# Gated linear attention on TensorE: state products with 64 rows per head in two banks instead of block-diagonal states

## The reference, cut to what matters

```
z = cumlogsumexp(s, axis=time);  g = exp(z_prev - z);  p = exp(s - z)
hk = hk * g + k (x) p            # state of 64 x 64 a head
ok = q . hk;  pv = softmax(ok)
hv = hv * g + p (x) v            # state of 64 x 128 a head
o = pv . hv
```

## Time and profile before

| | us |
|---|---|
| median of 3 runs (lowest, highest) | 891.55 (891.05, 891.7) |
| profiled execution, its own time | 890.84 |
| its span, slowest core (core 4) | 889.3 |
| even cores | 887.1 to 889.3 |
| odd cores | 856.3 to 859.7 |
| TensorE busy, core 4 | 845.4 |
| VectorE, ScalarE, GpSimd busy, core 4 | 364.0, 343.2, 150.8 |

### The profile page before, as it was taken

One profiled execution on the slowest core, in us unless ns is written; L12 is line 12 of the kernel. 1 busy time (PEld: TensorE's weight loads), 2 busy tenths in 40 slices (PEclk: granted clock), 3 DMA queues, 4 the chain that ended last, 5 costly groups with the idle time before them and its releaser, 6 DMA issues.

```text
span 889.3 us, 15119 instructions; the slowest of 8 cores (856.3 to 889.3 us)
## 1 busy us (share of the span) xinstructions
PE 845.4 (95%) x5521; PEld 455.7 (51%) x5585; DVE 364.0 (41%) x862; ACT 343.2 (39%) x746; POOL 150.8 (17%) x196
## 2 busy tenths in 40 slices
PE   3899999999999999999999999999999999999992
PEld 1344555555555555555555554444445666655540
DVE  1121244554555545454555554455553000023344
ACT  0111246555656456555655555101122222223333
POOL 6000012211222112112121222002112000001113
PEclk9899999999999999999999999999999999999997
DMA  8999902240422314221540226937703910005224
GB/s 136 161 171 169 162 1 48 49 83 14 96 48 48 65 32 95 49 48 28 116 95 1 84 56 172 268 87 136 149 1 77 181 29 1 1 14 129 95 95 193
DMA packets 13617, 77.46 MB, mean 87 GB/s; under 512 B 1632, under 2 KB 1632, under 8 KB 6624
## 3 DMA queue, kind: packets, MB, share of 16 engines
q0 software_dynamic: 9504, 57.51, 36.3%
q1 hardware_dynamic: 4032, 18.90, 5.5%
HBM read 124.47 MB, written 9.44 MB: 151 GB/s over the span
## 4 chain that ended last, share of the span: by engine, by line
PE 93%; DMA 2%; issue 2%; DVE 1%; ACT 1%; POOL 1%; POOLq 0%; DVEq 0%; ACTq 0%
PE p L246 64%; PE no L246 19%; PE tb L246 4%; PE aw L246 4%; DMA ws_a<-wsp 2%; PE st L246 1%; ACT sqd_a L293 0%; POOL xfm_a L300 0%; DVE x_a L266 0%; ACT mv_a L290 0%; POOL x_a L1208 0%; POOL ws_a L300 0%; POOLq L1348 0%; DVE x_a L1160 0%; DVE vx_a L266 0%
## 5 line engine op out<-in xcount | busy, mean ns | idle before, releaser
L246 PE MATMUL p<-s_a,xfm_a 128*128 128x512 bf16 x1117 | 253.0, 379 | 1.8
L246 PEld LDWEIGHTS p<-s_a,xfm_a 128*128 128x128 bf16 x1152 | 111.2, 98 | 123.9
L550 POOL TENSOR_TENSOR ng_a<-ng_a,gt_a 128x512 f32<-128x512 f32 x36 | 45.8, 1271 | 300.4 <-ACT gt_a L290 241.2
L246 PE MATMUL p<-x2fm_a,s_a 128*128 128x384 bf16 x512 | 87.5, 326 | 0.0
L266 DVE TENSOR_TENSOR awm_a<-aw,cbs 128x1024 bf16<-128x1024 f32 (+1 forms) x38 | 44.4, 1168 | 99.7 <-PE aw L246 99.7
L246 PE MATMUL p<-s_a,ofm_a 128*128 128x512 bf16 x341 | 78.2, 379 | 3.3 <-DVE x_a L266 2.8
L246 PE MATMUL p<-xfm_a,wq_a 128*128 128x384 bf16 x384 | 66.2, 326 | 0.0
L246 PEld LDWEIGHTS p<-x2fm_a,s_a 128*128 128x128 bf16 x512 | 48.4, 97 | 32.1 <-issue 0.6
L246 PE MATMUL p<-xfm_a,wk_a 128*128 128x384 bf16 x384 | 64.4, 326 | 0.0
L246 PEld LDWEIGHTS p<-s_a,ofm_a 128*128 128x128 bf16 x352 | 33.7, 98 | 40.7 <-issue 2.9
L246 PE MATMUL no<-s_a,ofm_a 128*128 128x512 bf16 x219 | 50.7, 379 | 0.3
(11 more groups left out here) (150 smaller groups left out, 1094.4 us busy)
## 6 DMA issues: line engine op xcount, KB each, us to landing
s_a<-w1p POOLq DMA_DIRECT2D x10, 1024.0 KB, 14.2
x_a<-x_main SPq DMA_DIRECT2D x9, 1024.0 KB, 12.2
s_a<-wvp POOLq DMA_DIRECT2D x8, 1024.0 KB, 17.1
s_a<-wgp POOLq DMA_DIRECT2D x8, 1024.0 KB, 11.9
s_a<-wop POOLq DMA_DIRECT2D x8, 1024.0 KB, 13.1
y<-x_a SPq DMA_DIRECT2D x16, 512.0 KB, 2.7
xfm_a<-xt_main POOLq DMA_DIRECT2D x12, 384.0 KB, 25.7
ws_a<-wsp POOLq DMA_DIRECT2D x8, 512.0 KB, 30.1
```

Source lines behind the costliest of these rows:

```text
L246: return t.matmul(out, lhsT, rhs, start=start, stop=stop, is_transpose=tp, skip_group_check=skip)
L550: g_tok[it] = gop(lambda e: e.tensor_tensor(b, b, gt.ap(0, 512), ALU.mult), [sg, n])
```

## The change

`s1bd` and `s2bd` become `s1` (128 columns) and `s2` (256 columns), in which the two heads of a pair lie below each other in the partitions and nothing is zero. The copies out of `st` become one instruction each. Each state product becomes two, of 64 rows of contraction, for the heads `e` = 0 and 1; these write to two banks. Numerators and denominators move from NP to `aw` (bank `e`, columns 0 to 127 and 128 to 255); the denominators become products of 128 columns, two for each before. The outputs use both banks of `no`. The instructions that read them take both banks with one access pattern, and the order of heads in `rr`, `okb`, `sm4` and `rs4` becomes that of the banks; the transposed order is undone in writing `cbf` and `ot`. `aw` is now freed by `sm_max` also, and both banks of `no` by `dve_ot`. The two `wo_unit` behind the loop use the two banks of `aw`.

```diff
-    s1bd = [small(f"s1bd{i}", 256, BF16) for i in range(2)]
-    s2bd = [small(f"s2bd{i}", 512, BF16) for i in range(3)]
+    s1 = [small(f"s1{i}", 128, BF16) for i in range(2)]
+    s2 = [small(f"s2{i}", 256, BF16) for i in range(3)]
...
-    for i in range(2):
-        z = v_set(s1bd[i].ap(0, 256), 0.0)
-    for i in range(3):
-        z = v_set(s2bd[i].ap(0, 512), 0.0)
...
-        a = v_copy(s1bd[b].ap3(0, [[128, 2], [1, 64]], 0, 64),
-                   bass.AP(ST, S1O, [[512, 64], [64, 2], [1, 64]]), w + [z])
-        a = v_copy(s1bd[b].ap3(64, [[128, 2], [1, 64]], 64, 64),
-                   bass.AP(ST, 64 * 512 + S1O, [[512, 64], [64, 2], [1, 64]]), w)
+        a = v_copy(s1[b].ap(0, 128), ST[:, S1O:S1O + 128], w)
...
+        q = s_copy(s2[it % 3].ap3(0, [[128, 2], [1, 128]]),
+                   bass.AP(ST, 0, [[512, 128], [S2O, 2], [1, 128]]), [m, a, o_mm.get(it - 3)])
...
     def pe_num_den(it):
         g, c = divmod(it, NM)
         b = it % 2
         eg = c * 1024 + g * GW
-        mm(NP[:, 256:512], lmask, em.ap(eg, 256), True, False, [t_e, t_cb] + fr(NP))
         before = c > 0 or NPF
-        if before:
-            mm(NP[:, 256:512], ones_bf, dg[b].ap(0, 256), False, False, [st_dg[it]])
+        for e in range(2):
+            mm(AW2[:, e * 512 + DEN:e * 512 + DEN + 128], lmask, em.ap3(eg + 64 * e, [[128, 2], [1, 64]]),
+               True, False, [t_e, t_cb] + fr(AW2) if e == 0 else [], skip=True)
+        for e in range(2 if before else 0):
+            mm(AW2[:, e * 512 + DEN:e * 512 + DEN + 128], ones_bf, dg[b].ap3(64 * e, [[128, 2], [1, 64]]),
+               False, False, [st_dg[it]] if e == 0 else [], skip=True)
         for p in range(2 if before else 0):
-            mm(NP[:, p * 128:(p + 1) * 128], kq[g % 2].ap((2 + p) * TM + c * 128, 128),
-               s1bd[b].ap(p * 128, 128), False, False, [st_s1[it]] if p == 0 else [])
-        for h in range(4):
-            p, e = divmod(h, 2)
-            tok = mm(NP[:, h * 64:h * 64 + 64], awm.ap(e * 512 + AOFF + p * 128, 128),
-                     em.ap(eg + h * 64, 64), False, h == 3, [a_tok[it]] if h == 0 else [], inc=(h == 3))
+            for e in range(2):
+                o = e * 512 + p * 64
+                mm(AW2[:, o:o + 64], kq[g % 2].ap((2 + p) * TM + c * 128, 128, 64 * e, 64),
+                   s1[b].ap(p * 64, 64, 64 * e, 64), False, False, [st_s1[it]] if p + e == 0 else [], skip=True)
+        for p in range(2):
+            for e in range(2):
+                o = e * 512 + p * 64
+                tok = mm(AW2[:, o:o + 64], awm.ap(e * 512 + AOFF + p * 128, 128),
+                         em.ap(eg + (2 * p + e) * 64, 64), False, True, [a_tok[it]] if p + e == 0 else [],
+                         inc=(p + e == 2), skip=True)
...
-        o1 = v_tt(okb.ap(0, 256), NP[:, 0:256], rr.ap(0, 256), ALU.mult, [r2, tok])
-        set_free(NP, o1, r2)
+        o1 = v_tt(okb.ap3(0, [[128, 2], [1, 128]]), pair(AW2, 0, 128), rr2, ALU.mult, [r2, tok])
+        set_free(AW2, o1, r2)
...
     def pe_outputs(it):
         before = it % NM > 0 or NPF
         for p in range(2 if before else 0):
-            mm(OB[:, p * 256:(p + 1) * 256], cT[it % 2].ap(p * 128, 128), s2bd[it % 3].ap(p * 256, 256),
-               p == 0, False, [st_s2[it], ct_tok[it]] + fr(OB) if p == 0 else [])
...
+            for e in range(2):
+                o = e * 512 + p * 128
+                mm(NO2[:, o:o + 128], cT[it % 2].ap(p * 128, 128, 64 * e, 64), s2[it % 3].ap(p * 128, 128, 64 * e, 64),
+                   p == 0, False, [st_s2[it], ct_tok[it]] + out_free["o"] if p + e == 0 else [], skip=True)
...
     dve_ot(last)
+    for half in AW:
+        set_free(half, *fr(AW2))
+    rot[0] = 1
     for _ in range(2):
         cc, n = wo_list.pop(0)
-        wo_unit(cc, n, gen[:3])[1]()
+        wo_unit(cc, n, AW)[1]()
+    for half in (NP, OB):
+        set_free(half, *out_free["o"])
     b_ot = pe_ot(last)
     act_of(last, b_ot)
```

More of the change, by code:

```diff
@@ L712, in dve_masks, with pair @@
             a_tok[ai] = t
+    DEN = 128
+    out_free = {"o": []}
+    def pair(h, lo, n):
+        return bass.AP(h, lo, [[1024, 128], [512, 2], [1, n]])
     def pe_num_den(it):
@@ L732, in emit @@
     ok3 = okb.ap3(0, [[64, 4], [1, 64]])
+    rr2 = rr.ap3(0, [[128, 2], [1, 128]])
     def sm_den(it, tok):
-        r1 = s_act(rr.ap(0, 256), NP[:, 256:512], AF.Ln, waits=[tok, c_tok.get(it - 1)])
+        r1 = s_act(rr2, pair(AW2, DEN, 128), AF.Ln, waits=[tok, c_tok.get(it - 1)])
         return s_act(rr.ap(0, 256), rr.ap(0, 256), AF.Exp, scale=-1.0, waits=[r1])
     def sm_max(it, tok, r2):
-        o1 = v_tt(okb.ap(0, 256), NP[:, 0:256], rr.ap(0, 256), ALU.mult, [r2, tok])
-        set_free(NP, o1, r2)
+        o1 = v_tt(okb.ap3(0, [[128, 2], [1, 128]]), pair(AW2, 0, 128), rr2, ALU.mult, [r2, tok])
+        set_free(AW2, o1, r2)
         o2 = v_red(mx4.ap(0, 4), ok3, ALU.max, [o1], negate=True)
@@ L747, in sm_end @@
     def sm_end(it, ex):
-        s1 = v_red(sm4.ap(0, 4), ok3, ALU.add, [ex])
-        s2 = v_rcp(sm4.ap(0, 4), sm4.ap(0, 4), [s1])
+        sr = v_rcp(sm4.ap(0, 4), sm4.ap(0, 4), [v_red(sm4.ap(0, 4), ok3, ALU.add, [ex])])
         s3 = v_tt(rr.ap(0, 256), okb.ap(0, 256), rr.ap(0, 256), ALU.mult, [ex])
-        c_tok[it] = v_tt(cbf.ap3(0, [[64, 4], [1, 64]]), rr.ap3(0, [[64, 4], [1, 64]]),
-                         sm4.ap3(0, [[1, 4], [0, 64]]), ALU.mult, [s2, s3, ct_mm.get(it - 1)])
+        c_tok[it] = v_tt(cbf.ap3(0, [[64, 2], [128, 2], [1, 64]]), rr.ap3(0, [[128, 2], [64, 2], [1, 64]]),
+                         sm4.ap3(0, [[2, 2], [1, 2], [0, 64]]), ALU.mult, [sr, s3, ct_mm.get(it - 1)])
     def pe_ct(it):
@@ L781, in pe_outputs @@
         for p in range(2 if before else 0):
-            mm(OB[:, p * 256:(p + 1) * 256], cT[it % 2].ap(p * 128, 128), s2bd[it % 3].ap(p * 256, 256),
-               p == 0, False, [st_s2[it], ct_tok[it]] + fr(OB) if p == 0 else [])
[L784 to L788, removed]
+            for e in range(2):
+                o = e * 512 + p * 128
+                mm(NO2[:, o:o + 128], cT[it % 2].ap(p * 128, 128, 64 * e, 64), s2[it % 3].ap(p * 128, 128, 64 * e, 64),
+                   p == 0, False, [st_s2[it], ct_tok[it]] + out_free["o"] if p + e == 0 else [], skip=True)
+        for p in range(2):
+            for e in range(2):
+                o = e * 512 + p * 128
+                tok = mm(NO2[:, o:o + 128], awm.ap(e * 512 + WOFF + p * 128, 128),
+                         vr[it % 4].ap((2 * p + e) * VS, 128), p == 0 and not before, True,
+                         [w_tok[it], v_tok[it]] + out_free["o"] if p + e == 0 else [], inc=(p + e == 2), skip=True)
         o_mm[it] = tok
@@ L792, in act_sq @@
     def act_sq(it, tok):
-        return s_act(sq.ap(0, 512), OB[:, :], AF.Square, waits=[tok, o_sq.get(it - 1)])
+        return s_act(sq.ap3(0, [[256, 2], [1, 256]]), pair(NO2, 0, 256), AF.Square, waits=[tok, o_sq.get(it - 1)])
     def dve_ms(it, q):
@@ L804, in dve_ot @@
         for h in range(4):
-            t = v_stt(ot.ap(h * 128, 128), OB[:, h * 128:(h + 1) * 128], rs4.ap(h, 1),
+            p, e = divmod(h, 2)
+            o = e * 512 + p * 128
+            t = v_stt(ot.ap(h * 128, 128), NO2[:, o:o + 128], rs4.ap(2 * e + p, 1),
                       ng[it % 2].ap(h * 128, 128), ALU.mult, ALU.mult,
                       [rs_tok[it], g_tok[it], oT_mm.get(it - 1)] if h == 0 else [])
-        set_free(OB, t)
+        out_free["o"] = [t]
         gate_done[it] = t
@@ L833, in emit @@
     NT = len(role.tiles)
+    out_free["o"] = fr(NP) + fr(OB)
     for p in range(2):
@@ L1058, in emit @@
     AL = ST
-    for half in AW:
-        set_free(half, *fr(AW2))
     first_g, second_g = role.groups
```

## The result

The changed kernel takes 899.34 us (median of 6 runs, 898.4 to 899.66), the kernel before 891.62 in the same comparison. The ratio is 1.0088, with a 95% interval of 1.0078 to 1.0098: a small loss, but clear of the noise. Forecast were 899.3 us and a slowdown. The profiled execution took 898.4 us.

What follows compares the result with a forecast made beforehand. TensorE's own sequence on the longer, even-numbered cores was taken as the bound. +8.7 us in the loop less 0.95 at the tail gives +7.7; with the median 0.7 above the profiled execution, 899.3 us, range 896.5 to 902.3.

Steps and rivals of the forecast that it cites:

- What a change of shape costs: On TensorE, each change of the array's shape costs 0.095 us, and the first group behind it 0.01 more.
- The form without a row, 64 rows by 64 columns: Numerators' four state products, a form missing from the profile rows: 0.07 us, between 0.05 and 0.12.
- An iteration: One loop iteration on TensorE grows 0.28 us: 0.16 in numerators and denominators, 0.12 in outputs; bounds 0.24 and 0.35.
- Iterations on the path: Of 32 iterations with each kind, one is hidden under TensorE's 1.77 us stall; 31 x 0.28 = +8.7 us.
- The tail: Behind the loop, output-projection units move to aw's banks, removing a 0.95 us wait after the transposes; later units unchanged.
- New waits: Numerators wait for the mask, later scores or weights for aw: no cost, with 2.2 and 2.7 us of cover.
- changes of shape are free among small products: Rival in the loop: changes cost nothing, only streaming counts; 5.6 us faster, 885.9 us; 7 in 100.
- the accumulating products don't pair: Rival in the loop: accumulating 64-row products don't run side by side; 0.43 us an iteration, 903.9 us; 4 in 100.
- the tail's stall stays: Rival behind the loop: ScalarE's copy of the transposes was the stall's true end; +8.7 us, 900.2; 8 in 100.
- part of the added time is hidden: Rival: part of the added time falls on hidden stretches, leaving the result within 0.2% (1.8 us); 3 in 100.

Runs made afterwards that it cites:

- grouped: Changed kernel with the 64-row products of numerators and outputs issued together, then both parts' score and weight products; two added changes of shape, not four; 1.0023 of the kernel before.
- interleaved: Changed kernel with the numerators' 64-row pairs alternating with their score products, six added changes of shape an iteration instead of four; ratio 1.0167 to the kernel before.
- one_half: Changed kernel with all state products of numerators and outputs taken from rows 0 to 63, same shapes, banks and number; ratio 1.0154 to the kernel before.
- full_array: Changed kernel's banks and number of products, but state products run over all 128 rows with block-diagonal states, no added changes of shape; ratio 0.999 to the kernel before.
- outputs_only: Changed kernel with 64-row products only in the outputs, the numerators back on the full array; ratio 1.0027 to the kernel before.
- numerators_only: Changed kernel with 64-row products only in the numerators, the outputs back on the full array; ratio 1.0069 to the kernel before.
- tail_banks: Kernel before, with only the two output-projection units behind the loop moved to the banks of aw; ratio 0.9993 to the kernel before.
- free_banks: Kernel before with the tail units in aw's banks and output-projection units of the last two iterations rotating over P0, P1 and NP; 887.65 us against 890.25.

## Why the prediction was right, point by point

- **What a change of shape costs.** Taken at 0.095 us and 0.01 for the first group behind it; measured 0.106 together from grouped and interleaved, and 0.105 from one_half against full_array. The added changes of one_half stand after products of 64 and of 128 columns, in numerators and outputs.
- **The form without a row, 64 rows by 64 columns.** Taken at 0.07 for four, between 0.05 and 0.12; from grouped 0.06 to 0.07. The bound 0.12 is what it costs without pairs (one_half: 0.22 with the change behind it).
- **An iteration.** 0.28 forecast, 0.270 measured (1252 - 982). The step was 0.01 too large, by the rounding of the timeline; 31 times, that is 0.3 us of the 8.7.
- **Iterations on the path.** The one of each kind under the stall was indeed hidden: the stall went from 1.77 to 1.50, by the 0.27 of that iteration. From the first scores to the last transposes 8.36 us were added, forecast 8.7.
- **The tail.** The 0.95 us went at their place. In the changed kernel 0.3 came back 40 us later, which I had said it would not:

```profile
616.41 0.69 DVE L266 TENSOR_TENSOR x_a<-no,x_a 128x512 f32<-128x512 f32 x1 [1.96 <-PE no L246]
617.55 0.69 DVE L1019 BATCH_NORM_STATS2 bst_a<-x_a 128x6 f32<-128x512 f32 x1 [0.45 <-DVE x_a L266]
...
621.20 0.61 PE L246 MATMUL tb<-cbs,scrb_a 128*128 128x128 bf16 x8 [0.15 <-POOL scrb_a L1029]
```

VectorE's statistics at 617.55 start 0.45 us after the eviction that they read, where 0.11 is usual, and the transposes at 621.20 wait for what follows from it. This is there on all even cores of the five kernels in which both parts use 64 rows, and in none of the others. The traces show that it goes with a place in VectorE's own program and not with banks or shapes. Behind a semaphore record VectorE's next instruction most often starts after 0.04 to 0.05 us. On the even cores of the eleven traces it starts 0.394 to 0.398 us behind it in 193 cases, and in 192 of them at places that are a multiple of 128 apart in the order of VectorE's records (semaphore records counted). The changed kernel has 38 such records fewer (1582, before 1620), and this moved one of the places to the statistics that the transposes wait for. outputs_only and numerators_only, with 1617 and 1585, have other instructions there. The kernel before has such gaps too, this one in the loop, where TensorE does not wait for VectorE:

```profile
365.20 0.43 DVE L266 TENSOR_TENSOR okb_a<-okb_a,mx_a 128x256 f32<-128x256 f32 x1 [0.46 <-DVE mx_a L281]
```

What VectorE does in these 0.35 us more the traces do not show.
- **New waits.** None: TensorE waits for no one in front of scores or numerators, and the copies that went from VectorE and ScalarE (0.28 us and 0.36 an iteration) bought nothing.
- **Rivals.** That changes of shape are free among small products is refuted by grouped and interleaved. That the accumulating products don't pair is refuted by one_half. That the tail's stall stays is refuted by tail_banks. That part of the added time is hidden is refuted by the 8.36 us, which are 31 x 0.270.

In the sum the errors nearly cancel, so the hit to 0.1 us is luck in part: 8.4 in place of 8.7, -0.6 in place of -0.95, and the difference of the medians is 7.7. That 0.3 us came back just here is luck altogether, since it hangs on the number of VectorE's instructions, which the forecast did not look at. What the trace of one core adds to that is the clock, below.

## What to carry to other kernels

Count the changes of the array's shape (128 rows to 64, 128 columns to 64, and back) in TensorE's order as if each were a product: here a change of rows costs 106 ns, about what one product of 256 columns takes (0.11 us), and a change of columns shows the same excess of 0.10 in the timelines. Halving the rows of a product pays only where what runs side by side saves more than the changes cost, or where the product lies next to others of the same shape. Here two changes cost 213 ns, and the pairs saved about 55 in the numerators and 110 in the outputs. And a copy saved on an engine that waits for TensorE is worth nothing: look for the places where TensorE waits, here two at the loop's end, worth 2.8 us for a few lines. A forecast to a few tenths of a us also has to allow for waits that move when the number of instructions changes.

## What was not expected of the hardware

The granted clock fell to half for a short stretch in some executions and on some cores, near small products or waits. In the changed kernel's trace it did so on cores 0, 2 and 4 near 868 us, behind the products with `aT` between which TensorE waits, and not on core 6. Core 0, then core 6, in the same stretch (PEclk is the granted clock):

```profile
core 0: us, PE busy (x) PEld busy (x) DVE busy (x) ACT busy (x) POOL busy (x), PEclk, DMA share, GB/s
...
868.00:871.40 3.40, 3.33 (x9) 1.17 (x9) 0.79 (x2) 0.00 (x0) 0.00 (x0) 0.50 0.00 0
```

```profile
868.00:871.40 3.40, 3.12 (x15) 1.39 (x16) 1.66 (x3) 0.00 (x0) 0.00 (x0) 1.00 0.00 0
```

In the stretch of 3.4 us core 0 ran at 0.50, that is 1.2 GHz, and its next group of products began 1.0 us later than it would have. From the last `ot` transposes to the end the changed kernel takes 318.9 us on the three cores with the fall and 318.0 on core 6. In the kernel before, core 2 shows it (319.7 us) and cores 0, 4 and 6 do not (318.5 to 318.8). About 1.0 us of it stands in the 0.30 us that the third stretch above grew by (-0.95 + 0.3 + 1.0, less rounding). The change isn't needed for it; whether it makes it more frequent, one profiled execution of each kernel cannot tell. The stall that free_banks takes away is a place of the same kind, as numerators_only showed with 1.7 us more behind it.
